# A raw buffer of its own for the output weights, their split in steps 2 and 3, and pitch 3 for the first half's probabilities

## The reference

```python
q = (x @ wq) -> 32 heads of 128;  k, v = (x @ wk), (x @ wv) -> 8 heads of 128
q = q * cos + rotate_half(q) * sin;  k likewise;  each k, v serves 4 q heads
att = softmax(mask(q @ k.T / sqrt(128)))
x = layernorm(x + (att @ v) @ wo)            # wo: 4096 x 512
nx = rmsnorm(x) * ln_w
x = layernorm(x + (silu(nx @ gate.T) * (nx @ up.T)) @ down.T)   # inner width 1792
```

## Time and profile before

| | |
|---|---|
| three runs, median (lowest, highest) | 1177.14 us (1176.69, 1178.65) |
| the profiled execution | 1178.0 us |
| its span, first to last instruction | 1176.2 us |
| TensorE busy | 1120.4 us (95%) |
| TensorE weight loads | 940.6 us (80%) |
| GpSimd busy | 835.4 us (71%) |
| VectorE busy | 817.6 us (70%) |
| ScalarE busy | 625.1 us (53%) |
| mean granted TensorE clock | 0.992 of full |
| SyncE's queue | 148.43 MB, 49.1% of the 16 engines' span |

### The profile page before, as it was taken

One profiled execution on the slowest core, in us unless ns is written; L12 is line 12 of the kernel. 1 busy time (PEld: TensorE's weight loads), 2 busy tenths in 40 slices (PEclk: granted clock), 3 DMA queues, 4 the chain that ended last, 5 costly groups with the idle time before them and its releaser, 6 DMA issues.

```text
span 1176.2 us, 18941 instructions
## 1 busy us (share of the span) xinstructions
PE 1120.4 (95%) x5346; PEld 940.6 (80%) x5346; DVE 817.6 (70%) x1416; ACT 625.1 (53%) x1122; POOL 835.4 (71%) x544
## 2 busy tenths in 40 slices
PE   7799999999999999999999999999997699999997
PEld 6588878887888788878878887888776588888885
DVE  6688787878787887788778778787888742222224
ACT  4565656666666666656665665666554332222224
POOL 3589978987897799689968997898765343343431
PEclk9999999999999999999999999999999899999999
DMA  6756555655564666566555555655555301111101
GB/s 189 206 152 155 136 139 143 160 138 138 141 166 119 162 156 160 128 157 157 142 139 140 150 133 144 156 147 129 134 141 129 112 19 53 53 54 53 53 0 72
DMA packets 148346, 148.75 MB, mean 126 GB/s; under 512 B 15200, under 2 KB 128864, under 8 KB 148320
## 3 DMA queue, kind: packets, MB, share of 16 engines
q1 hardware_dynamic: 148320, 148.43, 49.1%
HBM read 37.23 MB, written 2.10 MB: 33 GB/s over the span
## 4 chain that ended last, share of the span: by engine, by line
PE 78%; POOL 7%; issue 6%; DVE 4%; DMA 3%; ACT 2%; SPq 1%; POOLq 0%; DVEq 0%; ACTq 0%
PE ACC L1057 16%; PE ACC L1059 16%; PE ACC L1058 16%; PE S L1073 5%; PE S L1075 5%; PE S L1074 5%; PE S L1057 4%; PE S L1059 4%; PE S L1058 4%; DMA rope_s<-qk_raw 2%; POOL qk_raw L476 1%; POOL rope_s L477 1%; POOL Q_lo L486 1%; POOL PT_lo L502 1%; DVE turned L807 1%
## 5 line engine op out<-in xcount | busy, mean ns | idle before, releaser
L596 ACT ACTIVATE probs<-S,neg_max 128x128 f32<-128x128 f32 (+7 forms) x256 | 189.0, 738 | 213.2 <-DVE neg_max L796 212.6
L796 DVE CUSTOM_DVE_ANT_0 S<-S,mask 128x128 f32<-128x128 f32 (+7 forms) x256 | 194.1, 758 | 147.4 <-PE S L1075 147.3
L502 POOL TENSOR_TENSOR PT_lo<-PT_lo,PT_hi 128x896 fp32r<-128x896 f32 (+2 forms) x97 | 197.4, 2035 | 57.4 <-ACT PT_hi L603 57.4
L807 DVE STREAM_TRANSPOSE turned<-probs 128x128 f32<-128x128 f32 (+7 forms) x256 | 197.5, 772 | 1.7 <-ACT probs L596 1.6
L867 DVE SCALAR_TENSOR_TENSOR y<-ACC,row_rcp,y 128x512 f32<-128x512 f32 x256 | 177.2, 730 | 20.5 <-PE ACC L1059 20.5
L603 ACT ACTIVATE PT_hi<-PT_lo 128x1024 fp32r<-128x1024 f32 (+3 forms) x160 | 165.6, 1035 | 35.4 <-DMA PT_lo<-turned 34.6
L476 POOL TENSOR_TENSOR qk_raw<-qk_raw,cos_sb 128x512 f32<-128x512 f32 x76 | 128.0, 1685 | 45.2 <-DMA rope_s<-qk_raw 45.2
L1073 PE MATMUL S<-K_hi,Q_hi 128*128 (+5 forms) x384 | 134.5, 350 | 17.9 <-POOL Q_lo L486 13.8
L554 POOL TENSOR_TENSOR PT_lo<-rope_s,PT_hi 128x512 fp32r<-128x512 f32 x28 | 36.2, 1294 | 156.2 <-ACT PT_hi L735 156.2
L1057 PE MATMUL ACC<-PT_hi,V_hi 128*128 128x512 f32 (+3 forms) x384 | 134.6, 351 | 6.5 <-DVE PT_lo L814 5.9
L814 DVE TENSOR_TENSOR PT_lo<-PT_lo,PT_hi 128x1024 fp32r<-128x1024 f32 (+1 forms) x63 | 134.4, 2133 | 3.2
(11 more groups left out here) (128 smaller groups left out, 2574.7 us busy)
## 6 DMA issues: line engine op xcount, KB each, us to landing
PT_lo<-turned SPq DMA_DIRECT2D x256, 128.0 KB, 2.6
PT_lo<-turned SPq DMA_DIRECT2D x128, 208.0 KB, 3.7
rope_s<-qk_raw SPq DMA_DIRECT2D x160, 128.0 KB, 3.1
PT_lo<-turned SPq DMA_DIRECT2D x128, 112.0 KB, 2.6
PT_lo<-turned SPq DMA_DIRECT2D x128, 96.0 KB, 2.4
wq_raw<-in_L_attn_wq_dram SPq DMA_DIRECT2D x32, 256.0 KB, 3.2
wkvo_raw<-in_L_attn_wo_dram SPq DMA_DIRECT2D x32, 256.0 KB, 2.7
turned<-in_L_ffn_gate_w_t_dram SPq DMA_DIRECT2D x7, 512.0 KB, 3.9
```

The lines of the kernel that those rows point to most:

```text
L502: nc.gpsimd.tensor_tensor(lo, lo.bitcast(F32), hi.bitcast(F32), ALU.subtract).then_inc(pt_lo_done[half], 1)
L596: nc.scalar.activation(dst, src, ACT.Exp, bias=neg_max[:, at:at + 1], scale=-1.0, accum_out=row_sum[:, j % 2, i:i + 1]).then_inc(exp_done, 1)
L796: nc.vector.tensor_tensor_reduce(src, src, bias, scale=1.0, scalar=MASKED, op0=ALU.add, op1=ALU.min, accum_out=neg_max[:, at:at + 1]).then ...
L807: nc.vector.transpose(dst.rearrange("p b (r i) -> p r b i", i=QB), src.rearrange("p (r b i) -> p r b i", b=4, i=QB)).then_inc(turn_done, 1)
```

## The change

- `wkvo_raw` becomes two buffers, `wkv_raw` and `wo_raw`, with the waits that follow from that.
- SyncE loads `wo` in step 0, right behind `wq` (in head 0 in step 1, with no wait), in place of step 5.
- ScalarE makes `wo_hi` in step 2 in place of step 6, GpSimd `wo_lo` at the head of step 3 in place of step 7.
- The first half's probabilities have pitch 3: 13 units in place of 16. Tile 3 has four units, more than the pitch, and so the copies of tiles 2 and 3 run over seven units without a gap (128 x 896). The gap that is cleared shrinks.
- `act` moves to the buffers of the second half, which are large enough.

```diff
-PITCH = (4, 7)
-UNITS = (16, 29)
+PITCH = (3, 7)
+UNITS = (13, 29)
...
-        wkvo_raw = sb("wkvo_raw", [NC, HD])
+        wkv_raw, wo_raw = sb("wkv_raw", [NC, HD]), sb("wo_raw", [NC, HD])
...
-        act = [part(t[0], 0, (2, T)) for t in (PT_hi, PT_lo)]
+        act = [part(t[1], 0, (2, T)) for t in (PT_hi, PT_lo)]
...
-            if count == 1:
-                return units[:, :, at:at + rows, :].rearrange("p a r i -> p a (r i)")
+            if count == 1 or rows > PITCH[half]:
+                return units[:, :, at:at + (count - 1) * PITCH[half] + rows, :].rearrange("p a r i -> p a (r i)")
...
-            def load_wo(h, before, count):
-
-                sp.wait_ge(before, count)
+            def load_wo(h, count):
+
+                if count is not None:
+                    sp.wait_ge(wo_done, count)
                 wo_rows = wo[bass.ds(h * HD, HD), :].rearrange("p (c n) -> p c n", c=NC)
-                sp.dma_start(wkvo_raw[:], wo_rows).then_inc(wo_in, 16)
+                sp.dma_start(wo_raw[:], wo_rows).then_inc(wo_in, 16)
...
             for j, i in FIRST_HEAD:
-                if i == 5:
-                    load_wo(0, wkv_done, 2)
+                if i == 1:
+                    load_wo(0, None)
...
                     if i == 1 and j in (1, 3):
-                        sp.wait_ge(wo_done, g * REP + j)
+                        sp.wait_ge(wkv_done, g * 2 + (2 + j // 2))
                         w_v = wk_v if j == 1 else wv_v
-                        sp.dma_start(wkvo_raw[:], w_v[:, :, bass.ds(g * HD + HD, HD)]).then_inc(wkv_in, 16)
+                        sp.dma_start(wkv_raw[:], w_v[:, :, bass.ds(g * HD + HD, HD)]).then_inc(wkv_in, 16)
                     if i == 0:
                         load_wq(g * REP + (j + 2))
-                    if i == 5:
-                        load_wo(g * REP + j, *((wkv_done, g * 2 + (3 + j // 2)) if j % 2 else (wo_done, g * REP + j)))
+                    if i == 0:
+                        load_wo(g * REP + j, g * REP + j)
                     step(j, i)
...
-            for half, begin, end in ((0, 1, 4), (0, 11, 12), (1, 5, 7)):
+            for half, begin, end in ((0, 1, 3), (1, 5, 7)):
                 nc.gpsimd.memset(turned[half][:, :, begin * QB:end * QB], 0.0).then_inc(const_done, 1)
...
             def step(j, i, k_slot, last=False):
-                if i == 7:
+                if i == 3:
                     split_wo()
...
-                if i == 6:
-                    weight_hi("wo", wo_hi[:, n.n["wo"] % 2], flat(wkvo_raw), wo_in)
+                if i == 2:
+                    weight_hi("wo", wo_hi[:, n.n["wo"] % 2], flat(wo_raw), wo_in)
...
-            dve.wait_ge(const_done, 8)
+            dve.wait_ge(const_done, 7)
```

More of the change, by code:

```diff
@@ L315, in _ @@
                 if (half, begin) == (1, 0):
-                    sp.dma_start(wkvo_raw[:], wk_v[:, :, 0:HD]).then_inc(wkv_in, 16)
+                    sp.dma_start(wkv_raw[:], wk_v[:, :, 0:HD]).then_inc(wkv_in, 16)
                 cols = slice(half * HALF, (half + 1) * HALF)
@@ L321, in _ @@
             sp.wait_ge(wkv_done, 1)
-            sp.dma_start(wkvo_raw[:], wv_v[:, :, 0:HD]).then_inc(wkv_in, 16)
+            sp.dma_start(wkv_raw[:], wv_v[:, :, 0:HD]).then_inc(wkv_in, 16)
             def load_wq(h):
@@ L397, in _ @@
                     load_wq((GROUPS - 1) * REP + j + 2)
-                if i == 5:
-                    load_wo((GROUPS - 1) * REP + j, wo_done, (GROUPS - 1) * REP + j)
+                if i == 0:
+                    load_wo((GROUPS - 1) * REP + j, (GROUPS - 1) * REP + j)
                 step(j, i, last=True)
@@ L464, in split_wkv @@
                 hi, lo = (wo_hi[:, 1], wo_lo[:, 1]) if first else (flat(wkv_hi), flat(wkv_lo))
-                split("wkv", flat(wkvo_raw), hi, lo, wkv_in, wkv_done, both)
+                split("wkv", flat(wkv_raw), hi, lo, wkv_in, wkv_done, both)
             def split_wo():
                 slot = n.n["wo"] % 2
-                split("wo", flat(wkvo_raw), wo_hi[:, slot], wo_lo[:, slot], wo_in, wo_done)
+                split("wo", flat(wo_raw), wo_hi[:, slot], wo_lo[:, slot], wo_in, wo_done)
             def rope_sum(half, ago):
@@ L658, in step @@
                 if i == 3 and not last and j in (1, 3):
-                    weight_hi("wkv", flat(wkv_hi), flat(wkvo_raw), wkv_in)
+                    weight_hi("wkv", flat(wkv_hi), flat(wkv_raw), wkv_in)
                 if i == 5 and not (last and j >= REP - 2):
```

## The result

| | before | after |
|---|---|---|
| median of 16 runs each, in turn on one chip (lowest, highest) | 1177.72 us (1176.08, 1180.56) | 1180.41 us (1178.65, 1181.93) |
| the profiled execution, and its span | 1178.0, 1176.2 us | 1180.36, 1178.5 us |
| mean granted TensorE clock | 0.992 | 0.994 |

The ratio of after to before is 1.0022, with a 95% interval of 1.0015 to 1.0030: 2.7 us slower (1.8 to 3.5). The interval does not touch 1, and its middle lies at the 0.2% that a measurement of this kernel can tell from no change: a loss that is real and small. I forecast +4.6 us.

What follows compares the result with a forecast made beforehand. TensorE makes up 78% of the chain, so edits count only where it waits. A 0.78 us stall in head 2, net 0.67 a pass over seven passes, less 0.13, gives +4.6: 1181.7 us, range 1177.0 to 1186.0.

Steps and rivals of the forecast that it cites:

- The place and the mechanism: Head 2, step 7: wo_lo ahead of GpSimd's low parts makes TensorE wait about 0.8 us before PV, seven times.
- The stall's size: Head 2: 1.29 us for wo_lo, less 0.29 by pitch and 0.22 usable spare, gives 0.78 us a pass.
- What comes back: Head 3: a 0.11 us wait for Q_lo vanishes each pass; the last pass has 0.13 us more to spare.
- The total: Whole kernel: 7 x 0.67 - 0.13 = +4.6 us, bounds +3.2 to +6.6.
- the likeliest case: Whole kernel: the forecast of 1181.7 us, with its own range 1180.0 to 1184.5 and chance 0.60.
- The pitch: GpSimd's low part of tiles 2 and 3: 128x896 takes 2.13 us against 2.42, 0.29 less.
- The load: SyncE, step 0: 256 KB ahead of the rotation transfers; halves land at 532.3, wanted at 532.86, so nothing.
- The margin that the locked product gives: Head 2: GpSimd's product excludes VectorE's subtraction, so one ready as late as 533.9 ends no later.
- The start: Head 0: waiting for wo ahead of the probabilities only reorders waits; 0 us, bounds 0 and +1.7.
- A, late rotations: Head 2, every pass: rotation lands 0.5 us too late, 3.5 us on top, so 1185; chance 0.13.
- B, no stall: Head 2: GpSimd's list gets its 0.78 us elsewhere, so the time is 1177; chance 0.15.
- C, faster by transfers set free: Head 1: moving the wo load speeds tiles 4 and 5's transfers, shortening Q_lo waits; about 1170.7; chance 0.12.

Runs made afterwards that it cites:

- e3: Changed kernel with GpSimd's wo_lo moved from the head of step 3 to step 5, behind the low part of tiles 2 and 3; 1177.23 us, 0.9999 of before.
- e4: Changed kernel with the wo_lo subtraction made twice in step 3; 1192.14 us, ratio 1.0119 to before.
- e8: Kernel before with the rotation transfers issued by ScalarE instead of SyncE, nothing else; 1180.28 us, ratio 1.0015 to before.
- e1: Kernel before with only the pitch of 3 and what goes with it, the weights as they were; 1176.41 us, ratio 0.9994 to before.
- e2: Changed kernel with wo_hi back in step 6 and wo_lo back in step 7, the load still early; 1178.11 us, ratio 1.0006 to before.
- e5: Changed kernel with the copies of tiles 2 and 3 back at 128x1024, pitch and places kept; 1181.8 us, ratio 1.0038 to before.
- e10: Changed kernel with wo_lo in step 5 behind the low parts and only step 5's Q rotation issued by ScalarE; 1169.64 us, ratio 0.9923 to before.

## Why the prediction was right, and where its sizes were off

**The place and the mechanism** held: a wait for GpSimd's PT_lo before PV in step 7 of head 2, seven times, nowhere else of note. e3 takes it away by moving one instruction, e4 nearly triples it, and the time follows. The forecast delay of PV was 0.78 us; by starts it is 0.65, of which the rows show 0.49 to 0.51 as idle time. One reading of the waits was not quite right: two of the 11 waits for Q_lo (0.31 and 0.14 us) are in head 2, not in head 1 or the last group.

**The stall's size.** The forecast was 7 x 0.78 - 0.13 = 5.33 us at its place; measured 4.65. Two terms were too large. The instruction was priced by its duration, 1.29 us; in a list without gaps the next one starts 1.24 to 1.26 us after it (538.93 to 540.17), 0.04 less, 0.28 in seven passes. The hand-over was taken as 0.12 us from Q_lo to the scores; here it is 548.71 - 548.65 = 0.06, 0.42 in seven passes. The 0.12 belongs to another reader, the scores behind Q_lo (in e8 again, 454.76 to 454.90, 0.14). The sum of both is 0.70, and 5.33 - 0.70 = 4.63.

**What comes back** was too small: 0.77 us forecast, 1.6 measured. The forecast's own term was right in size: up to step 3 of head 3 the segment is 0.83 us shorter, since in before the first score there waited for Q_lo in six of seven passes (up to 0.14 us late at its start and 0.1 us more at the next), in after in one. What it lacked is a second small wait of the same kind, right behind: PV of the second half in step 3 of head 3. In before VectorE's low part ends 0.05 to 0.09 us ahead of it in every pass (227.95 for 228.01), in after 0.47 to 0.95 ahead in six of seven (228.14 for 228.62). The wait shows in the distance to the next matmul, 0.33 us against 0.22 (VectorE and TensorE, before, then after):

```profile
225.73 2.22 DVE L814 TENSOR_TENSOR PT_lo<-PT_lo,PT_hi 128x1024 fp32r<-128x1024 f32 x1
...
228.01 0.50 PE L1057 MATMUL ACC<-PT_hi,V_hi 128*128 128x512 f32 x1
228.34 0.39 PE L1058 MATMUL ACC<-PT_lo,V_hi 128*128 128x512 f32 x1
```
```profile
225.91 2.23 DVE L815 TENSOR_TENSOR PT_lo<-PT_lo,PT_hi 128x1024 fp32r<-128x1024 f32 x1
...
228.62 0.39 PE L1058 MATMUL ACC<-PT_hi,V_hi 128*128 128x512 f32 x1
228.84 0.40 PE L1059 MATMUL ACC<-PT_lo,V_hi 128*128 128x512 f32 x1
```

That is most of the 0.76 us in the segment up to step 7 of head 4. The segments bear it out in the other kernels: from step 3 of head 3 to step 7 of head 4 it is 301.7 to 302.0 us in before, e1, e2 and e3, and 301.1 to 301.2 in after, e4 and e5, which have the stall.

**The total.** So +3.2 us at the loop's end, of which the profiled execution shows 2.3 in its span by the chance of the clock told above; the runs say 2.7, with 1.8 to 3.5. That slowdown lies under the forecast's own lower bound for the sum, +3.2, which only its interval reaches. The median, 1180.41, does lie within the likeliest case's 1180.0 to 1184.5, 1.3 us under the 1181.7, but with some luck: the forecast stood on a median of 1177.14 for before, which is 1177.72 over the 16 runs, and on the old one 2.7 us would have given 1179.8.

**The pitch** saves 0.29 us a pass: 2.40 against 2.11 in the rows, 0.29 in e5's segment, none in e1, where nobody waits. Taken as forecast.

**The load** is hidden (e2). The second transfer landed at 533.98, or 532.3 if after's delay of 1.7 us by then is taken off, which is the 532.3 that I had. The margin that the locked product gives was not needed, but the lock shows again: VectorE's subtraction ends at 532.98 + 2.22 = 535.20, and the product begun at 534.08 ends at 536.35, 1.15 us later, as it did before (533.99 and 535.14).

```profile
532.98 2.22 DVE L815 TENSOR_TENSOR PT_lo<-PT_lo,PT_hi 128x1024 fp32r<-128x1024 f32 x1
```

By the rule that the prediction cites, from the Trainium skill's "SBUF — State Buffer", section "Who interferes with whom", the second waits for the end of the first; both kernels' traces agree.

**The start** was taken as 0 and is -0.07 us, less than executions differ by. TensorE's idle time moved forward, as forecast: it waits 2.88 us at 40.56 in place of 2.43 at 44.17, with the half clock moved alike.

**The waits of head 1.** Q_lo is unchanged (13.8 and 13.7 us). VectorE's add is waited for 2.0 us more, which I had not forecast, but the segment that holds both has grown by 0.16 us only: the later wait had been partly paid for by another.

**The rivals.** A, late rotations: no wait for rope_s ahead of the product in head 2, and e2 has the early load at no cost. B, no stall: the seven waits. C, faster by transfers set free: the head-1 wait would have had to shrink, and neither after nor e2 shrinks it. The path that C pointed at was the right one for a gain, though: with the late Q's rotation issued by ScalarE and not behind SyncE's transfers of tiles 4 and 5, the waits for Q_lo in head 1 fall from 1.4 to under 0.2 us (e10).

## What to carry to other kernels

On an engine that issues its list without a gap, the price of a moved instruction is its distance to the next start, less the spare of the first reader behind it that TensorE waits for; so look for the tightest reader behind the new place before moving anything, and put the instruction behind that reader, not ahead of it. A saving is worth its size only where someone waits: the same 0.29 us was worth nothing in one kernel and 2 us in the next. And follow the largest wait that TensorE still has back to the queue that holds it: moving one pair of transfers in each head to another engine's queue gave 8 to 9 us, three times what the change had lost.

## What the hardware showed that was not expected

- Right behind two of e4's seven waits of 1.4 us TensorE's clock fell to its lower level (0.57 of full over 444 to 448), which made the following segment 1.57 us longer. As long a wait in head 1 (1.25 to 1.43 us, 49 of them in seven kernels) never did that in the loop, nor did 1.59 us in e8. So a stall can cost more than itself, and its length alone doesn't tell whether it will.
- A matmul that starts after a wait is followed by the next one later than without: at the start of PV in step 7 after 0.34 us (548.71 to 549.05), where the same place without the wait has 0.28 to 0.29; at the start of PV in step 3 after 0.33 (228.01 to 228.34) against 0.22. So each wait costs 0.05 to 0.11 us beside its length.
- A wait can hide in the table: with modelled ends, VectorE's low part held PV in step 3 of head 3 by about 0.1 us in every pass of before, and no idle time is shown. The start right behind the producer's end (0.05 to 0.09 us) gives it away.
- Two rotation transfers issued 2.2 us earlier, from ScalarE, let the product start only 0.6 to 1.4 us earlier. The issue of the second took 1.32 to 1.51 us there, against 0.60 to 1.05 on SyncE, and ScalarE's next work waited for it.
- 256 KB more ahead of two transfers of 128 KB in one queue made the first land 0.4 us later after its issue and the second 1.1 us (3.9 against 2.8), which is what the bytes take at the rate of the window; over the seven passes the second's delay is 0.4 to 1.1 us.
